# The gate's token operand goes through DRAM: the turned tokens are stored once and loaded back

## What is computed

```
q = silu(dwconv(x @ Wq)); k = silu(dwconv(x @ Wk)); v = silu(dwconv(x @ Wv))
beta = sigmoid(x @ Wb)
delta = delta_rule(l2norm(q), l2norm(k), v * beta, k * beta, chunk=32)
paths = [fir3(v), fir15(v), fir64(v), delta, v]              # 5 paths, 4 heads of 64
stats = [mean, mean of squares, mean of |.|, norm] of each path and head   # 80 numbers for a token
gate_in = concat([x, stats (each repeated 64 times)])
probs = softmax((gelu(gate_in @ gW1 + gb1) @ gW2 + gb2) / tau)
x1 = layernorm(x + rmsnorm(sum(probs * paths)) * norm_w @ Wo)
```

## Time and profile before

| | |
|---|---|
| runs | 971.75, 963.71 and 973.4 us; median 971.75 |
| the profiled execution | 971.51 us, of which the trace's span is 969.7 us |
| busy, share of the span | PE 89%, PE weight loads 67%, DVE 63%, ACT 47%, POOL 36% |
| traffic | 123.52 MB by DMA, 127 GB/s on the mean |
| instructions | 18401 |

### The profile page before, as it was taken

How to read it: one execution, slowest core, us unless ns; L and a number is a source line. 1 busy time by engine, 2 the same in 40 slices (tenths; PEclk the granted TensorE clock), 3 DMA queues, 4 the chain that set the end, 5 groups by cost and what they waited for, 6 DMA issues and landing times.

```text
span 969.7 us, 18401 instructions
## 1 busy us (share of the span) xinstructions
PE 863.9 (89%) x6886; PEld 648.7 (67%) x6886; DVE 607.3 (63%) x1410; ACT 451.7 (47%) x845; POOL 344.7 (36%) x336
## 2 busy tenths in 40 slices
PE   8897789779999986998899889989997999999994
PEld 6665566667777765786566556556785777777774
DVE  6998697576889988533567786774462343333255
ACT  5777555446666655442244534445331323222221
POOL 8422200123557566312001352233540242222684
PEclk9999899798999987999799999999999999999998
DMA  6799669897655432124991112002202222221421
GB/s 196 206 281 286 164 157 252 294 222 183 123 120 122 77 76 65 46 87 160 388 353 42 63 64 89 18 23 98 78 23 85 65 66 66 58 65 50 152 66 65
DMA packets 144468, 123.52 MB, mean 127 GB/s; under 512 B 89790, under 2 KB 126590, under 8 KB 143102
## 3 DMA queue, kind: packets, MB, share of 16 engines
q1 hardware_dynamic: 140974, 112.98, 41.8%
q0 software_dynamic: 3408, 9.38, 2.6%
HBM read 74.04 MB, written 48.29 MB: 126 GB/s over the span
## 4 chain that ended last, share of the span: by engine, by line
PE 56%; DVE 15%; ACT 10%; DMA 6%; POOL 5%; SPq 4%; issue 4%; POOLq 0%; DVEq 0%; ACTq 0%
PE ps L2527 10%; PE ps L1933 5%; PE ps L2542 5%; DVE cross_room L1966 3%; PE ps L2391 3%; PE ps L1873 3%; PE ps L1366 3%; PE ps L681 3%; PE ps L1634 3%; PE ps L437 2%; PE ps L1995 2%; POOL kept L2674 2%; PE ps L2404 2%; DMA hank<-rt_dram 2%; PE ps L1518 2%
## 5 line engine op out<-in xcount | busy, mean ns | idle before, releaser
L2011 ACT ACTIVATE cross_room<-ps 128x1024 f32<-128x1024 f32 x64 | 65.5, 1023 | 98.5 <-PE ps L1937 98.5
L2527 PE MATMUL ps<-wr,xbT 128*128 x312 | 99.0, 460 | 2.0 <-ACT xbT L2563 2.0
L1966 DVE TENSOR_REDUCE cross_room<-ps 128x4 f32<-128x1024 f32 x64 | 78.0, 1223 | 35.8 <-PE ps L1933 35.0
L1933 PE MATMUL ps<-kept,cross_room 32*128 32x256 f32 x512 | 74.5, 413 | 20.0 <-DVE cross_room L1966 18.4
L2616 POOL DMA_INDIRECT y_dram<-yb,dest_row x39 | 37.4, 960 | 133.4 <-DVE dest_row L2592 129.2
L1334 POOL TENSOR_TENSOR st<-st,exponent 128x20 f32<-128x20 f32 x16 | 56.8, 3548 | 62.4 <-DVE st L1309 61.1
L2527 PEld LDWEIGHTS ps<-wr,xbT 128*128 128x128 f32 x312 | 58.8, 189 | 29.6 <-issue 2.7
L1937 PE MATMUL ps<-cross_room,kept 32*128 32x256 f32 x512 | 75.6, 414 | 0.0
L1933 PEld LDWEIGHTS ps<-kept,cross_room 32*128 32x128 f32 x512 | 47.3, 191 | 37.9 <-issue 18.4
L565 DVE SCALAR_TENSOR_TENSOR room<-room 128x256 f32<-128x256 f32 x144 | 58.3, 479 | 9.7 <-ACT room L514 9.7
L2601 DVE TENSOR_TENSOR cross_room<-cross_room,ps 128x352 f32<-128x352 f32 x39 | 20.3, 521 | 58.8 <-PE ps L2527 58.8
(11 more groups left out here) (355 smaller groups left out, 2234.5 us busy)
## 6 DMA issues: line engine op xcount, KB each, us to landing
xs_dram<-params SPq DMA_DIRECT2D x17, 1040.0 KB, 17.9
room<-in_gW SPq DMA_DIRECT2D x8, 1280.0 KB, 8.9
tok_dram<-room SPq DMA_DIRECT2D x8, 768.0 KB, 6.7
fir_dram<-room SPq DMA_DIRECT2D x6, 1024.0 KB, 7.3
paths<-fir_dram SPq DMA_DIRECT2D x48, 128.0 KB, 3.7
xb<-xs_dram SPq DMA_DIRECT2D x39, 130.0 KB, 2.4
hank<-rt_dram SPq DMA_DIRECT2D x8, 512.0 KB, 8.4
yr<-y_dram SPq DMA_DIRECT2D x16, 256.0 KB, 3.1
```

Source lines behind the costliest of these rows:

```text
L1933: m1 = nc.tensor.matmul(ps[:, c, t * T:(t + 1) * T], strips(qS[b % 3], g, c)[:, t * P:(t + 1) * P], kS(b, g)[c * CH:(c + 1) * CH], start=T ...
L1966: V.tensor_reduce(mx[:, :, g, XD + 2 * h * CH:XD + (2 * h + 1) * CH + 1:CH].rearrange("p t c -> p c t"), ps[:, pair(h), :].rearrange("p c ...
L2011: S.activation(pT[g % 2][:, pair(h)].rearrange("p c k t -> p (c k t)"), ps[:, pair(h), :].rearrange("p c n -> p (c n)"), ACT.Exp).then_inc ...
L2527: m = nc.tensor.matmul(ps[:, 2 * (j % 2) + half, 0:FF], xbT[j % 2][:, k, :], wr[:, bass.ds(e, 1), k, half, :].rearrange("p e n -> p (e n)" ...
```

## The change

In the Project phase SP stores `xT` of each batch to a new DRAM tensor `xT_dram` (eight stores of 256 KB), in the third round of the project stage. ACT's copy of the next batch into `xT` now waits until the store of the last one has landed, since there is one `xT`. In the gate, SP loads `x_gate` from `xT_dram`, already turned; the four transposes, ACT's copy to `dxT` and that tile are gone, and the matmuls of L1366 read `x_gate` itself. The buffer is therefore held until these matmuls are done (`hid_made`) and not only until the transposes are.

```diff
         def sp_project(b):
             i = b % 2
-            for _ in range(5):
+            for _ in range(2):
+                yield
+            sp.wait_ge(s.xT_copied, b + 1)
+            nc.sync.dma_start(env.xT_dram[b], flat(xT[:])).then_inc(*s.xT_out.up(16))
+            for _ in range(3):
                 yield
             sp.wait_ge(s.sums_copied, b + 1)
...
         def act_copy_x(b):
             act.wait_ge(s.xT_turned, b + 1)
             act.wait_ge(s.beta_made, b)
+            act.wait_ge(s.xT_out, 16 * b)
             S.copy(xT[:].rearrange("p k t -> p (k t)"), ps[:, 0, :]).then_inc(*s.xT_copied.up())
...
-        x_gate = [sb(f"dx_gate{i}", [P, TT, D]) for i in range(2)]
+        x_gate = [sb(f"dx_gate{i}", [P, KT, T]) for i in range(2)]
         x_res = [sb(f"dx_res{i}", [P, TT, D]) for i in range(2)]
-        xT = sb("dxT", [P, KT, T])
...
         def sp_statistics(b):
             i = b % 2
-            sp.wait_ge(s.gx_turned, b - 1)
-            nc.sync.dma_start(x_gate[i][:], batch(a["x"], b)).then_inc(*s.x_gate_in[i].up(16))
+            sp.wait_ge(s.hid_made, 2 * (b - 1))
+            sp.wait_ge(fir.xT_out, 16 * B)
+            nc.sync.dma_start(flat(x_gate[i][:]), env.xT_dram[b]).then_inc(*s.x_gate_in[i].up(16))
             yield
...
         def pe_gate(b):
-            i = b % 2
-            pe.wait_ge(s.x_gate_in[i], 16 * (b // 2 + 1))
+            xT = x_gate[b % 2]
             pe.wait_ge(s.lgT, b)
             pe.wait_ge(s.stat, 6 * b + 6)
             pe.wait_ge(s.norm, 2 * b + 2)
-            for c in range(KT):
-                for t in range(TT):
-                    m = nc.tensor.transpose(ps[:, 6, (c * TT + t) * P:(c * TT + t + 1) * P], x_gate[i][:, t, c * P:(c + 1) * P], ident[:])
-            m.then_inc(*s.gx_turned.up())
             pe.wait_ge(s.gate_step, STEPS * (b - 1) + 2)
             for t in range(TT):
                 m = nc.tensor.transpose(ps[0:80, 7, t * P:(t + 1) * P], st[:, t].rearrange("p s n h -> p (s n h)"), ident[:])
             m.then_inc(*s.st_turned.up())
             yield
-            pe.wait_ge(s.gxT, b + 1)
+            pe.wait_ge(s.x_gate_in[b % 2], 16 * (b // 2 + 1))
             pe.wait_ge(s.stT, b + 1)
...
         def act_gate(b):
-            act.wait_ge(s.gx_turned, b + 1)
             act.wait_ge(s.hid_made, 2 * b)
-            S.copy(flat(xT[:]), ps[:, 6, :]).then_inc(*s.gxT.up())
             act.wait_ge(s.st_turned, b + 1)
             S.copy(stT[:], ps[0:80, 7, 0:T]).then_inc(*s.stT.up())
             yield
...
         env.tok_dram = nc.dram_tensor("tok_dram", [B, P, TT * 3 * D], F32).ap()
+        env.xT_dram = nc.dram_tensor("xT_dram", [B, P, KT * T], F32).ap()
```

More of the change, by code:

```diff
@@ L245, in phase_project_invert_and_fir @@
     V, S, G = nc.vector, nc.scalar, nc.gpsimd
-    s = pg.signals("Project", "wq_in wk_in wv_in wb_in taps_in wpad_zero wpad raw_zero sel_zero sel_made filters_turned filters_copied filters_out xT_turned xT_copied raw_made raw_copied beta_made tanh beta first mac silu "
+    s = pg.signals("Project", "wq_in wk_in wv_in wb_in taps_in wpad_zero wpad raw_zero sel_zero sel_made filters_turned filters_copied filters_out xT_turned xT_copied xT_out raw_made raw_copied beta_made tanh beta first mac silu "
                    "sums_made sums_copied small_zero conv_turned sq v_copied ss rn_step tok kT_turned kT_copied a_made diag win_zero win_made fir_made stage_copied small_in tau_log eps_exp small",
@@ L859, in phase_delta_and_gate @@
         "lT z1_made z gw1_made gw g2 x1_turned x1 z2_made gw2_made vb u0_made w_made wTn uT u0_turned u s_made sbd u1_made u1_turned "
-        "cleared o_made oT path_turned dl sq stat norm gx_turned gxT st_turned stT hid_made gelu lg_made lgT lg_turned gate_step ex "
+        "cleared o_made oT path_turned dl sq stat norm st_turned stT hid_made gelu lg_made lgT lg_turned gate_step ex "
         "mix osq rms on on_turned onT y_made y_add bn rstd applied fir_in0 fir_in1 fir_in2",
```

## The result

The changed kernel takes 980.82 us (median of 20 runs, 969.03 to 986.17), the kernel before 971.62 us on the same chip (20 runs, 963.71 to 982.41). The ratio is 1.0082, with a 95% interval of 1.0059 to 1.0106: slower by 8 us. A second set of runs gave 1.0079 (1.0029 to 1.0128). The profiled execution of the changed kernel is one of its slower ones (986.17 us, span 984.3), so the two spans are not subtracted here.

The account below looks back on a forecast made before the run. The prediction took Project as bound by its full DMA queue, and the middle gate steps by DVE's weighing and ACT, not PE. Its sum, 9.6 + 2.0 - 2.8 = +8.8 us on 971.51, gave 980.3 us, range 970 to 989.

Parts of the forecast that it names:

- The stores' place in the queue and ACT's wait: Project: stores land behind weight rows and filter DMAs, ACT's next copy waits; batch 7's projections +9.6 us, 3.8 from step 2.
- The shift goes through whole: After Project: its last batch issues or releases what follows, so the whole delay of its projections passes on.
- The size beside this one profile: End of Project: batch 7's projections move from 100.82 to 110.4 us, the filters' matmuls come 10 to 12 us later.
- The clock, +2.0: Project: PE runs at a lower clock after waits before batches 2 and 7, 1.0 us each, +2.0 us.
- The gate, -2.8: Gate: removed transposes and copies gain 2.8 us in the last three batches, nothing in batches 0 to 4.
- the three places: Gate of batches 5, 6 and 7, where the chain runs through transposes or copy: gains of 1.0, 1.3 and 0.5 us.
- the rival in which PE is the bound: Gate: PE bounds it, so 32 transposes save 10 us and the kernel takes 962 us; chance 0.05.
- The rival built on it: Project: stores don't wait for DMAs ahead, landing some 3 us after issue; 970.7 us, no change; chance 0.18.
- landings come in the order of issue: SP's queue in Project: each DMA lands only when everything issued ahead of it has landed.
- The third rival: Project: waits keep SP from issuing, so stalls add up to 23 us, time 992 us; chance 0.13.
- The chances: Whole kernel: within 1% of before 0.54, slower 0.41, faster 0.05.

Follow-up runs that it names:

- e3: Kernel before (old gate) plus eight 256 KB stores of a never-changing weight tile, without ACT's wait: ratio 0.9965 to the kernel before.
- e4: Changed kernel with the old gate and each store cut to 8 KB, ACT still waiting: ratio 1.0042 to the kernel before.
- e7: Changed kernel with each store at the head of SP's next step, ahead of token load, weight rows and filters: ratio 0.9997 to the kernel before.
- e5: The changed kernel unaltered, run again: ratio 1.0079 to the kernel before.
- e1: Changed kernel with the old gate put back, keeping the 256 KB stores and ACT's wait: ratio 1.0052 to the kernel before.
- e2: Changed kernel's new gate alone, without stores or ACT's wait, loading the input unturned: ratio 0.9966 to the kernel before.
- e12: e2 a second time, new gate without stores or wait: ratio 0.9999 to the kernel before.
- e6: Changed kernel with stores of a never-changing weight tile and no ACT wait; the gate reads xT_dram back: ratio 1.0009 to the kernel before.
- e10: e6 a second time, new gate, weight-tile stores, no ACT wait: ratio 1.0013 to the kernel before.
- e8: Changed kernel with each store issued from ACT's own queue, right behind its copy: ratio 1.011 to the kernel before.
- e9: Like e6, but the gate loads the input instead of xT_dram: ratio 0.9959 to the kernel before.
- e11: e3 a second time, old gate, weight-tile stores, no ACT wait: ratio 0.9959 to the kernel before.

## Why the prediction was right, and where it was not

The forecast was +8.8 us and the runs gave +9.2 (980.82 - 971.62); on the ratio, +8.0. The mechanism of the larger part was right. Two terms were off in opposite directions, the waits with their clock too dear and the gate's gain too large, so that the sum comes this close is in part luck.

**The stores' place in the queue and ACT's wait: right.** e3 and e4 separate it from the traffic, e7 removes it by order alone. "The shift goes through whole" was right too. The last projection matmul starts at 110.5, 109.7, 114.3 and 112.0 us in the four profiles in which the store stands mid-queue and ACT waits for it (the changed kernel, e5, e1, e4), 111.6 on the mean, and at 99.9 to 106.2 in the nine without such waits, 102.5 on the mean. That is 9.1 us. (e7, 107.7, is in neither group: there the token load stands behind the store, and the tokens of batches 6 and 7 take 6.3 and 6.5 us to land. Counted with the nine it would make the difference 8.6 us. So in this one profile the store's new place moved part of the delay to the tokens; its twelve runs show no loss.) At the last filter matmul the two means are 9.0 us apart, at the gate's first output projection 8.7. Forecast: 9.6.

**The size beside this one profile: not borne out.** Batch 7's projections went from 100.82 to 105.03, +4.2 and not +9.6, and the last filter matmul came 1.9 us later, not 10 to 12. The step that failed is the base: the sum took the landings of one execution for those of the kernel, and Project was late in it. Its last projection matmul, at 106.2, is the latest of the nine; e2 and e12, whose Project is that of the kernel before, have it at 100.4 and 104.0. Before, then after, read by the line of the projections:

```profile
L437 PE MATMUL ps<-room,weights x192: 377/378/792, 5.6 to 106.2; 128*128 128x256 f32 x192
```

```profile
L441 PE MATMUL ps<-room,weights x192: 377/378/787, 5.8 to 110.5; 128*128 128x256 f32 x192
```

Its DMA engines were as busy as in others and moved less: from 48 to 60 us 278 GB/s where e3 moved 303. The window from 156 to 164 us of the kernel before, then of e3, in the filters:

```profile
156.00:164.00 8.00, 6.46 (x73) 4.05 (x66) 7.42 (x18) 3.85 (x5) 0.00 (x0) 1.00 1.02 266
```

```profile
156.00:164.00 8.00, 8.00 (x102) 7.00 (x98) 7.39 (x18) 5.25 (x7) 0.00 (x0) 1.00 0.98 357
```

266 against 357 GB/s at a share of 1.0, and PE idles a fifth of the window in the one and not in the other.

**The clock, +2.0: right in kind, in another place, and too much on top.** It was put before batches 2 and 7. In the changed kernel's profile it fell at batches 5 and 6 (3.68 us in place of 1.90, twice), in e1's at batches 2 and 5 (3.37 and 3.60 us), in e5's at batch 5 (3.78). The 9.1 us between the two groups of profiles hold it already. The two terms together were 11.6 us; the runs say 7 (e5 less e6) to 8.5 (e1 less e3), and only 5 if e1 is set beside the kernel before.

**The gate, -2.8: wrong in sum.** No pair of kernels shows it safely, and the profiles show none of it. From the first output projection (the gate's) to the last, the five profiles with the old gate take 167.1 to 168.7 us, 167.9 on the mean, and the nine with the new one 167.5 to 169.0, 168.2 on the mean. The chain shows what became of the three places. The chain that ended last, before, then after:

```profile
339.32 0.65 PE ps L1080 x32
...
354.23 1.93 PE ps L1518 x8
...
364.51 1.11 PE ps L1245 x4
...
367.51 8.24 PE ps L1366 x24
...
376.50 0.59 ACT delta_room L1532
...
387.13 4.37 PE ps L1366 x12
391.50 3.46 PE ps L1634 x16
394.95 1.73 PE ps L1640 x8
```

```profile
346.37 0.65 PE ps L1084 x32
...
360.93 1.92 PE ps L1516 x8
...
370.93 1.13 PE ps L1249 x4
...
373.13 7.48 PE ps L1366 x24
...
381.37 0.59 ACT delta_room L1530
...
391.51 5.46 PE ps L1366 x12
396.97 3.90 PE ps L1632 x16
400.87 1.73 PE ps L1638 x8
```

The lag of the lower list behind the upper is 7.05 us at the first row, 6.70 at the second, 6.42 at the third, 5.62 at the fourth, 4.87 at the fifth, 4.38 at the sixth and 5.92 at the last. Batch 5 gave 0.35 us, and 0.28 by the third row, in place of 1.0, because DVE's weighing took the transposes' place on the chain (the row at 347.93 above). Batch 6 gave 1.55 (forecast 1.3), but only 0.80 of it by what is gone: the other 0.76 is that its 24 matmuls of L1366 took 7.48 us in place of 8.24. Batch 7 gave 0.49 (forecast 0.5), and right behind it the same matmuls took 1.1 + 0.4 us longer. The windows there, before and after:

```profile
384.00:388.00 4.00, 0.87 (x2) 0.82 (x3) 3.90 (x6) 2.83 (x7) 3.69 (x4) 0.85 0.21 67
```

```profile
389.00:393.00 4.00, 1.86 (x6) 1.25 (x5) 3.92 (x5) 2.96 (x6) 3.62 (x5) 0.50 0.22 68
```

The matmuls behind the wait for ACT ran at half clock for longer. Of 2.67 us saved on the chain by then (7.05 - 4.38) 1.54 were given back at once.

The other profiles show two ways through this stretch. In five of the nine with the new gate (the changed kernel, e2, e5, e10, e12) the last gate's 12 matmuls take 5.46 us. In four of the five with the old gate they take 4.37 to 4.52, but there the 24 of the gate before take longer, and in e1 they take 5.46 too. Taken together, the 24, the 12 and the 16 of L1634 take 16.1 to 16.6 us in the five profiles with the old gate and 16.1 to 17.0 in these five, 16.2 and 16.7 on the means: half a microsecond given back, and not 1.5. In the other four with the new gate (e6, e7, e8, e9) the 12 take 4.43 to 4.45, but the eight matmuls of the output projection ahead of them take 3.73 us in place of 1.94, which no profile with the old gate has. In e6:

```profile
368.62 3.73 PE ps L1516 x8
...
379.19 4.45 PE ps L1366 x12
```

From the first output projection to the last these four take 169.0 us on the mean, the other five 167.6 and those with the old gate 167.9. So where PE runs slowly moved with the gate. That the missing transposes move it is argued: no run put other work of PE in their place.

PE saved 10 us of transposes and the kernel is no faster for it. That speaks against the rival in which PE is the bound (its 962 would be 0.99).

**The rule on the order of landings.** What the prediction quoted of the Trainium skill ("DMA: Bandwidth & Descriptors", section "Queues, rings and completion order"), that completion is "not FIFO per issuing engine", has a case in the changed kernel's trace. The store issued at 77.96 us and a filter DMA of 56 KB on 16 partitions issued behind it, at 79.18:

```profile
xT_dram<-room SPq DMA_DIRECT2D x1, 256.0 KB, 11.8
hank<-rt_dram SPq DMA_DIRECT2D x1, 56.0 KB, 9.1
```

The later one lands at 88.3, the store at 89.8. So the rule holds here, by 1.5 us; no view used here shows on how many DMA engines the later one ran. The rival built on it fell all the same: stores landed in a median of 8 us, not 3. The statement that landings come in the order of issue was too strong; that they come about when what is ahead has landed is what the sum needed.

**The third rival**, stalls that add up, is out. ACT stood still for 18.9 us in all before e1's copies and 15.4 in the changed kernel, and the projections moved by 9 (the two groups of profiles above).

**The chances.** The interval (1.006 to 1.011) lies across the bound of 1% at which "same" and "slower" were parted; 0.54 and 0.41 were fair.

## What to carry to other kernels

A DMA whose landing gates an engine costs by its place in the queue, not by its bytes: 8 KB cost what 256 KB did, and with the store first in its step no loss shows. Work taken off an engine can be missing from the time because other stretches then run at its lower clock: read the instructions around the place, and in more than one profile, since one pair put at 1.5 us what five of each put at 0.5. And before a sum is built on landings of one execution, look at how far such times move between executions. Here the last projection matmul moved by up to 3.6 us between two profiles of one kernel (e2 and e12) and by 6 over the nine, on a term of 9.6.

## What the runs showed of the hardware that was not expected

The mean granted clock, listed for each run, goes with the gate and not with the stores. It is 0.9585 on the mean of 147 runs with the old gate (99 of the kernel before in the three sessions of experiments, 48 of e1, e3, e4 and e11; standard error 0.0005) and 0.9550 over 104 runs with the new one (the changed kernel's 20, and e2, e5, e6, e7, e9, e10, e12; 0.0007; e8's six, at 0.944, are left out and would lower it). Between runs of the same kernel 0.01 of clock goes with 6.5 us, so 0.0035 would be 2.3 us, about what the gate should have gained. This is a correlation that fits the slow stretches in the gate; that it is the cause is not shown.

One stretch takes one of two courses. Where the delta rule's first batches run, around 205 to 225 us, the clock was near 1.0 in some executions and 0.5 in others, worth about 5 us from the last filter matmul to the first output projection (89.2 us on the mean of the eight low profiles, 84.0 on that of the other six). The changed kernel:

```profile
210.00:215.00 5.00, 4.83 (x30) 3.81 (x30) 5.00 (x5) 2.12 (x9) 3.89 (x2) 0.50 1.06 209
215.00:220.00 5.00, 5.00 (x60) 3.91 (x58) 3.94 (x5) 1.37 (x4) 3.17 (x1) 0.50 0.91 197
```

The low course was seen in 6 of 9 profiles with the new gate and in 2 of 5 with the old, too few to tell them apart.

Eight stores that nobody needs (e3, e11) made the kernel before faster twice, by 0.4% with intervals that just exclude 1. Neither trace shows a reason; it stays open. No version run here beats both kernels and still computes the gate from the stored tokens; e7 comes nearest, at the time of the kernel before.
